# A quantised projection and a LoRA MLP on one core: gate/up and down as two-by-two block multiplications with seven block products

## The reference, cut to what matters

```python
# x: 8 x 256 x 1024, that is 2048 tokens of 1024; all float32
w_eff = quantise(weight + delta, codebook) * scale + delta      # 1024 x 1024, delta = lora_B @ lora_A / 2
x = x + x @ w_eff.T
gate = x @ W_gate.T + 0.5 * (x @ A_gate[idx].T) @ B_gate[idx].T  # W_gate, W_up: 2752 x 1024, rank 16
up   = x @ W_up.T   + 0.5 * (x @ A_up[idx].T)   @ B_up[idx].T    # idx: one adapter for each batch of 256 tokens
act  = silu(gate) * up
x = x + act @ W_down.T + 0.5 * (act @ A_down[idx].T) @ B_down[idx].T   # W_down: 1024 x 2752
```

## Time and profile before

| | |
|---|---|
| median of 3 runs | 1862.82 us (1861.52 to 1865.01) |
| span of the profiled execution | 1864.1 us; no other time is recorded for it |
| PE busy | 1810.1 us, 97% of the span |
| DVE busy | 746.1 us, 40% |
| ACT busy | 419.4 us, 22% |
| POOL busy | 72.6 us, 4% |
| DMA moved | 154.93 MB |

### The profile page before, as it was taken

How to read it: one execution, slowest core, us unless ns; L and a number is a source line. 1 busy time by engine, 2 the same in 40 slices (tenths; PEclk the granted TensorE clock), 3 DMA queues, 4 the chain that set the end, 5 groups by cost and what they waited for, 6 DMA issues and landing times. The chain is left out here.

```text
span 1864.1 us, 23210 instructions
## 1 busy us (share of the span) xinstructions
PE 1810.1 (97%) x8129; PEld 1466.2 (79%) x8129; DVE 746.1 (40%) x1261; ACT 419.4 (22%) x891; POOL 72.6 (4%) x76
## 2 busy tenths in 40 slices
PE   6799999999999999999999999999989999999998
PEld 5578877888888888888888888888776787778776
DVE  6989848533333333333333333332463111211221
ACT  5422243222222222122222222221232111111110
POOL 4820000000000000000000000000000000000000
PEclk9999999999999999999999999999999999999999
DMA  6584465111111111111111111110365243323431
GB/s 201 141 183 128 125 214 164 50 50 46 47 49 49 49 49 47 44 45 49 49 49 44 49 49 49 50 47 23 98 172 165 52 115 93 98 60 87 107 85 50
DMA packets 222225, 154.93 MB, mean 83 GB/s; under 512 B 92064, under 2 KB 193440, under 8 KB 222048
## 3 DMA queue, kind: packets, MB, share of 16 engines
q1 hardware_dynamic: 207680, 125.95, 25.3%
q10 hardware_dynamic: 12416, 22.55, 3.3%
q0 software_dynamic: 2080, 5.80, 1.6%
HBM read 102.34 MB, written 57.70 MB: 86 GB/s over the span
## 5 line engine op out<-in xcount | busy, mean ns | idle before, releaser
L1253 DVE TENSOR_TENSOR av<-bankU,sg 128x512 f32<-128x512 f32 x84 | 58.1, 691 | 561.8 <-PE bankU L1363 561.8
L1351 PE MATMUL bankG<-xh,wh 128*128 128x512 f32 x704 | 278.8, 396 | 1.6 <-PEq L290 1.6
L1688 PE MATMUL bankS<-dn_h,ah 128*128 128x512 f32 x704 | 279.7, 397 | 0.5 <-DVE ah L1635 0.5
L1688 PE MATMUL bankS<-dn_l,ah 128*128 128x512 f32 (+1 forms) x704 | 278.5, 396 | 0.0
L1351 PE MATMUL bankG<-xh,wl 128*128 128x512 f32 x704 | 275.5, 391 | 0.0
L1351 PE MATMUL bankG<-xl,wh 128*128 128x512 f32 x704 | 275.1, 391 | 0.0
L1688 PE MATMUL bankS<-dn_h,al 128*128 128x512 f32 x672 | 262.9, 391 | 0.0
L1351 PE MATMUL bankU<-xl,wh 128*128 128x512 f32 x672 | 262.2, 390 | 0.0
L1351 PE MATMUL bankU<-xh,wl 128*128 128x512 f32 x672 | 262.0, 390 | 0.0
L1351 PE MATMUL bankU<-xh,wh 128*128 128x512 f32 x672 | 262.0, 390 | 0.0
L1635 DVE TENSOR_TENSOR al<-a_raw,ah 128x256 fp32r<-128x256 f32 x168 | 71.0, 423 | 306.2 <-ACT ah L1572 306.1
(11 more groups left out here) (158 smaller groups left out, 1942.4 us busy)
## 6 DMA issues: line engine op xcount, KB each, us to landing
act_d<-av ACTq DMA_DIRECT2D x84, 256.0 KB, 2.4
a_raw<-act_d SPq DMA_DIRECT2D x168, 128.0 KB, 2.5
wn<-in_L_cond_W_gate_dram SPq DMA_DIRECT2D x84, 128.0 KB, 2.9
wn<-in_L_cond_W_up_dram SPq DMA_DIRECT2D x84, 128.0 KB, 2.8
wn<-in_L_cond_W_down_dram SPq DMA_DIRECT2D x42, 256.0 KB, 3.3
xnat<-in_x_dram SPq DMA_DIRECT2D x8, 1024.0 KB, 5.1
x1T_d<-x1t_st SPq DMA_DIRECT2D x32, 256.0 KB, 2.5
x_d<-x1n_st SPq DMA_DIRECT2D x32, 256.0 KB, 2.8
```

What stands on the lines that cost most here:

```text
L1253: dv.tensor_tensor(av[0:rows, :], up, sg[0:rows, :], ALU.mult).then_inc(s_av, 1)
L1351: te.matmul(bank[:, :], a[:, q, g, k, :], b[:, c, k, :], start=(k == 0 and n == 0), stop=False)
L1688: last = te.matmul(bank[par][NH * t + h][:, :], a[0:r, slot, tok], w[0:r, k, cols], start=(k == 0 and m == 0), stop=False)
```

## The change

Gate, up and down are each computed as a two-by-two block product with seven block products in place of eight. For gate and up the blocks are halves of the 2752 weight rows (1376 each: 11 tiles, the last of 96 rows), halves of the 1024 inputs, and two chunks of 512 tokens out of four. For down they are halves of the 2752 inputs, of the 1024 outputs and of the tokens. The block sums are made in float32 ahead of the split into high and low:

- Sums of x1's blocks (XS_d): on VectorE at the end of stage 1 for the first token half (`pair_sums`), on GpSimd in stage 2 for the second (`xt_sums`).
- Sums of weight blocks: four on GpSimd for every pass of seven products (`w_s12`, `w_s3`, `w_s4`).
- Sums of the act blocks (`act_sum`, four for two passes) and of W_down's blocks (`dn_sums`, four for each of 11 tiles) on GpSimd too. Act blocks and sums go to LT_d (seven operands), W_down's to RT_d.

A pass `mm` is one weight (gate for m = 0, up for m = 1) by one of 11 tiles by one half of the tokens: 44 passes, a pair is `it` (22). In a pass the position `p` counts the products; product p is 12 matmuls into its own bank, and four of the seven also get an adapter matmul. VectorE adds the banks up in SBUF (`ev`, L1405 to L1421), which it did not do before: silu and the product of gate and up then read SBUF. The split weights go through a ring of five (`rh`, `rl`); the weight transposes go to SBUF (`wt`). W_down is transposed by VectorE in stage 2 (`dn_tr`, L1389), so stage 3 has no transposes on TensorE. x1 is no longer transposed back in stage 1: VectorE transposes it from XR_d in stage 3 (`residual`, L1757). Stage 2 now loads its x1 operands from HBM, seven of 1 MB for each token half, which `x_hi` and `x_lo` split; in the first pass of each half TensorE also computes the adapters' inputs (`T`, 16 and 24 matmuls) and VectorE `make_ts`. The act buffer and W_down are read back in stage 3, in 14 runs of 11 steps; each run is a product for one half of the tokens, 12 matmuls a step, and `evict` adds its four banks into one to four blocks of the result, which is in SBUF throughout. The loops of stages 1 to 3 are now written out.

```diff
-                        for tt in range(TT):
-                            last = te.transpose(bankM[:, tt * P:(tt + 1) * P], x1t_st[:, c % 2, tt * P:(tt + 1) * P], ident[:, :])
-                        last.then_inc(s_trM, 1)
...
-                        for k in range(KD):
-                            if k % TT == 0 and c == 0 and not (isinstance(j, int) and j == 0):
-                                pe.wait_ge(s_lo, use(j, 2 * g + k // TT) + 1)
-                            for n, (a, b) in enumerate(((wh, xh), (wh, xl), (wl, xh))):
-                                te.matmul(bank[:, :], a[:, q, g, k, :], b[:, c, k, :], start=(k == 0 and n == 0), stop=False)
...
-                            for m in range(TT):
-                                last = te.transpose(bank[1][wbank(k, h)][0:r, m * P:(m + 1) * P], dn_n[:, h, m, 0:r], ident[:, :])
-                            last.then_inc(s_dntr, 1)
...
-                                    for m, (a, w, r) in enumerate(pairs):
-                                        last = te.matmul(bank[par][NH * t + h][:, :], a[0:r, slot, tok], w[0:r, k, cols],
-                                                         start=(k == 0 and m == 0), stop=False)
-                            last.then_inc(s_used, 1)
...
+            OUT = (bank1[:, :], bankA[:, 1, :], bankA[:, 0, :], bank7[:, :], bank5[:, :], bankC[:, 1, :], bankC[:, 0, :])
...
+                    def w_s12(mm):
+                        rows = rows_of(mm // 2 % NJ)
+                        gp.wait_ge(s_tr, 4 * mm + 3)
+                        wait(gp, s_lo, 7 * (mm - 1) + 5)
+                        tt(wsrc(S1, rows), wsrc(L21, rows), wsrc(L22, rows), ALU.add).then_inc(s_sum, 1)
+                        gp.wait_ge(s_sum, 4 * mm + 1)
+                        tt(wsrc(S2, rows), wsrc(S1, rows), wsrc(L11, rows), ALU.subtract).then_inc(s_sum, 1)
...
+                        gp.wait_ge(s_sum, 4 * mm + 2)
+                        tt(wsrc(L12, rows), wsrc(L12, rows), wsrc(S2, rows), ALU.subtract).then_inc(s_sum, 1)
...
+                            ins = tt(s1a[r, :], a12, a22, ALU.add)
...
+                            ins = tt(s2a[r, :], s1a[r, :], a11, ALU.subtract)
...
+                            tt(b11, b12, b11, ALU.subtract).then_inc(s_ds, 1)
...
+                    def hi(v):
+                        mm, p, it, m = split(v)
+                        rows = rows_of(it % NJ)
+                        s, n = ((s_tr, 1), (s_sum, 2), (s_tr, 4), (s_sum, 3), (s_sum, 1), (s_tr, 3), (s_sum, 4))[p]
+                        act.wait_ge(s, 4 * mm + n)
+                        wait(act, s_pd, v - RING + 1)
+                        nc.scalar.copy(rh[:, v % RING, 0:KH * rows], wsrc(RSRC[p], rows)).then_inc(s_hi, 1)
...
+                        dv.transpose(wsrc(n, rows), src).then_inc(s_tr, 1)
+                    def lo(v):
+                        mm, p, it, m = split(v)
+                        rows = rows_of(it % NJ)
+                        dve.wait_ge(s_hi, v + 1)
+                        dv.tensor_tensor(rl[:, v % RING, 0:KH * rows], wsrc(RSRC[p], rows),
+                                         rh[:, v % RING, 0:KH * rows].bitcast(f32), ALU.subtract).then_inc(s_lo, 1)
...
+                        dv.transpose(dt_[r, b, :], src.rearrange("p a r -> p (a r)")).then_inc(s_dtr, 1)
...
+                                dv.tensor_tensor(e[:, 0:2, :], bankA[r, :, :], tm[r, None, :].to_broadcast([r.stop, 2, CH]),
+                                                 ALU.add).then_inc(s_ev, 1)
...
+                                dv.tensor_tensor(e[:, 2, :], bank7[r, :], e[:, 1, :], ALU.add).then_inc(s_ev, 1)
...
+                                dv.tensor_tensor(e[:, 1:4:2, :], bank5[r, None, :].to_broadcast([r.stop, 2, CH]), e[:, 1:3, :],
+                                                 ALU.add).then_inc(s_ev, 1)
...
+                                dv.tensor_tensor(e[:, 1:3, :], bankC[r, :, :], e[:, 1:3, :], ALU.add).then_inc(s_ev, 1)
...
+                    def product(u, ks, first, signal):
+                        mm, p, it, m = split(u)
+                        rows = rows_of(it % NJ)
+                        last = None
+                        for k in ks:
+                            cols = slice(k * rows, (k + 1) * rows)
+                            for n, (a, b) in enumerate(((rh, xh), (rh, xl), (rl, xh))):
+                                last = te.matmul(OUT[p][0:rows, :], a[:, u % RING, cols], b[:, OPND[p], k, :],
+                                                 start=first and k == ks[0] and n == 0,
+                                                 stop=k == KH - 1 and n == 2 and p in (0, 1, 3))
...
+            PORD = (M7, M5, M6, M1, M2, M4, M3)
+            C11, C12, C21, C22 = range(4)
+            TARGETS = {M7: (C21, C22), M5: (C12, C22), M6: (C12, C21, C22), M1: (C22, C11, C12, C21),
+                       M2: (C11,), M4: (C21,), M3: (C12,)}
...
+            RES_RUN = (8, 8, 4, 4, 4, 4)
...
+                    for k in range(NJ):
+                        load_r(0, k)
+                        if k < NL:
+                            load_l(k)
+                        if k == NL:
+                            sp.dma_start(td[:, :, :].bitcast(f32), TD_d.rearrange("c p n -> p c n")).then_inc(s_td, 16)
+                            for n in range(4):
+                                sp.dma_start(bd[n * CR:(n + 1) * CR, :, :].bitcast(f32),
+                                             BdT_d[n // 2].rearrange("(c r) d -> r c d", r=CR)).then_inc(s_bd, 16)
...
+                    def load_res(n):
+                        q, h, t = RES[n]
+                        wait(act, s_res, n - 1)
+                        for g in range(NI):
+                            for e in range(2):
+                                i = 2 * (q % 2) + e
+                                act.dma_start(xs[g * Q:(g + 1) * Q, n % 2, e * KD:(e + 1) * KD, :],
+                                              XR_d[2 * h + q // 2, :, i * Q:(i + 1) * Q, t * P + g * Q:t * P + (g + 1) * Q]
+                                              .rearrange("o c r -> c o r")).then_inc(s_xs[n % 2], 16)
...
+                    nres = 0
+                    for k in range(NJ):
+                        r_hi(0, k)
+                        if k < NL - 1:
+                            l_hi(k)
+                    act.wait_ge(s_bd, 64)
+                    nc.scalar.activation(bdn[:, :, :], bd[:, :, CH:D].rearrange("p (h t) n -> p h t n", t=2)[:, :, 1, :].bitcast(f32),
+                                         ACT.Copy, scale=-1.0).then_inc(s_bdn, 1)
...
+                        dv.transpose(c_tile(q, h, t), xs[:, n % 2, :, :].rearrange("p b r -> p (b r)")).then_inc(s_res, 1)
...
+                        for q in TARGETS[PORD[r // 2]]:
+                            c = c_tile(q, r % 2, t)
+                            ins = dv.tensor_tensor(c, bank[r % 2][t][:, :], c, ALU.add)
+                        ins.then_inc(s_ev, 1)
...
+                    pe.wait_ge(s_td, 16)
+                    pe.wait_ge(s_bdn, 1)
+                    for n in range(NJ * NRUN):
...
+                            for i, (a, b) in enumerate(((lh, rh), (lh, rl), (ll, rh))):
+                                last = te.matmul(out_, a[0:rows, n % NL, tok], b[0:rows, k, :],
+                                                 start=(k == 0 and i == 0), stop=(k == NJ - 1 and i == 2 and not adds))
...
```

More of the change, by code:

```diff
@@ L398, in _ @@
                     tile(0)
-                    with sp.Fori(0, 2) as i:
+                    for i in range(2):
                         tile(2 * i + 1)
@@ L693, in _ @@
                     adapters(0)
-                    with dve.Fori(0, 2) as i:
+                    for i in range(2):
                         for q in (0, 1):
@@ new lines, in lora @@
+                    def lora(u):
+                        mm, p, it, m = split(u)
+                        h, rows = it // NJ, rows_of(it % NJ)
+                        half, t = {2: (0, 0), 4: (1, 1), 5: (1, 0), 6: (0, 1)}[p]
+                        pe.wait_ge(s_ts, 2 * h + t + 1)
+                        pe.wait_ge(s_bs[m], 128 * (it + 1))
+                        te.matmul(OUT[p][0:rows, :], bs[:, m, t, half * P:half * P + rows], ts[:, t, m, :],
+                                  start=False, stop=True).then_inc(s_pd, 1)
@@ new lines, in _ @@
+                    for n in range(NJ * NRUN):
+                        r, k = n // NJ, n % NJ
+                        if n + NL < NJ * NRUN:
+                            load_l(n + NL)
+                        if r % 2 == 1 and r // 2 + 1 < NRUN // 2:
+                            load_r(r // 2 + 1, k)
+                        if r - 1 in FINAL and k in (2, 4, 6, 8):
+                            store(r - 1, k // 2 - 1)
+                    for t in range(TT):
+                        store(NRUN - 1, t)
@@ new lines, in _ @@
+                    for k in range(NJ):
+                        r_lo(0, k)
```

(16 more changed lines are left out.)

1609 lines of the change are left out of this document (835 added, 774 removed).

## The result

The changed kernel takes 1968.34 us (median of 4 runs, 1964.68 to 1970.33) against 1863.36 (4 runs, 1861.52 to 1865.01): ratio 1.056, 95% interval 1.054 to 1.058. It is 5.6% slower; 1748 was forecast, so the forecast is 220 us off and on the wrong side. The profiled execution took 1963.1 us.

What follows compares the result with a forecast made beforehand. It took the time as a count of TensorE instructions: 256 + 49 + 2 + 928 + 20 + 12 = 1267 us to stage 2's end, + 41 + 3 + 424 + 8 + 5 = 1748, 6.2% faster; range 1700 to 1832.

Steps and rivals of the forecast that it cites:

- TensorE's count: Matmuls at 0.2247 us each: 4128 in stage 2 (928 us) and 1888 in stage 3 (424 us).
- Loss 49: Seam into stage 2: 78 us to the end of pass 0, its matmuls worth 29; bounds 25 and 65.
- Store and barrier 5: Seam into stage 2: storing x1's last block and the barrier behind it take 5 us.
- 20 us lost: Between the token halves: operand work and masking of adapter sums fall on two passes; bounds 5 and 35.
- I charge 12 us over the whole stage: Stage 2: 12 us for pairs in which VectorE's and GpSimd's bursts don't fit together.
- 8 us of ring: Stage 2: five weight slots let VectorE be late by three products, 8 us.
- 41 us: Seam into stage 3: additions, `td`, store, barrier and the wait for `bdn`, where there were 3.7; bounds 30 and 55.
- the neighbour: GpSimd beside VectorE in stage 2: each GpSimd instruction costs VectorE 0.55 us; bank readers would go free.
- B: Rival, stage 2: VectorE partly the bound, 3 to 5 us more for 15 pairs, 1800 to 1830; chance 0.22.
- D: Rival, stage 2: each GpSimd instruction delays VectorE 1.08 us, bank readers and transposes too; 171 us, 1907 in all; chance 0.08.
- That seven products don't show: Rival: matmuls stand further apart as 12 in place of 24 go to a bank between waits; no difference, 0.01.
- The signs I had named: Stage 2: right, 440 or more matmuls in 100 us; wrong, under 420 with TensorE waiting for L1307, or slowed bank readers.

Runs made afterwards that it cites:

- kernel 1: The changed kernel with each down-adapter step `td` one product later on TensorE: 1858.69 us, ratio to before 0.997.
- Kernel 4: The changed kernel with x operands and the second load of A issued earlier on SyncE at the start of stage 2: 1952.41 us.
- Kernel 11: kernel 5 plus Kernel 4's order, the down stage's adapter operands loaded in the eighth step, the residual's loads issued by GpSimd: 1797.33 us, ratio to before 0.966.
- kernel 2: The changed kernel with GpSimd's block sums in stage 2 narrowed to 8 columns after the first passes, result incomplete: 1905.39 us.
- kernel 6: kernel 1 with GpSimd's block sums of stage 2 narrowed to 8 columns after the first passes, result incomplete: 1819.82 us.
- kernel 13: The changed kernel with five more matmuls ahead of each `td` outside the first and the middle pass: 1963.51 us.
- kernel 5: kernel 1 with all work on W_down (loads, transposes, sums, stores) four products later: 1816.03 us, ratio to before 0.976.

## Why the prediction was wrong

The forecast missed the profiled 1963.1 us by 215. Where they are, step by step, with a matmul at 0.2247 us:

- **TensorE's count** (4128, or 928 us, for stage 2 and 1888, or 424 us, for stage 3) was right, and so was its price: 442 start in 100 us in kernel 1.
- **Stage 1** ended its matmuls at 260.4, forecast 256: 4 us.
- **"Loss 49"** for the seam into stage 2 (51 with the clock): 79, so 28 us. Two terms were too small. "Store and barrier 5": from the last matmul of stage 1 (260.4) to the first load of stage 2 (280.54) 20 us pass, in which SyncE still loads and stores for the sums of x1's blocks. No run here touched it. And SyncE's order: I had the queue as a list of issues in time and not as instructions that wait. `store_bs` waits for `bh` and `bl`, the weight load of pass 2 for a transpose, and x and A stand behind them. Kernel 4 shows 16 us of it.
- **"20 us lost"** between the token halves: 100 us with 265 matmuls lose 40, so 20 us. 18.9 of the 40 are again `td`'s waits for `al`, up to 6.3 us long. Kernel 11 still loses 38 there, mostly in waits for `ts`, A and `al`, and no run was aimed at it: its cause stays open.
- **"I charge 12 us over the whole stage" is the step that failed.** Steady stage 2, from 400 to 860 and from 960 to 1478, has 978 us for 3610 matmuls worth 811: 167 us lost, 155 above the charge. The charge compared each engine's load in a pair with 41.3 us (and its own upper ends, 42 and 43 us, are above that). The loads fit, and VectorE stayed at 68%. But `td` is an instruction in TensorE's order with a chain of six steps on VectorE and ScalarE behind the product ahead of it, and one product, 2.8 us, to cover it; the prediction put this wait at nothing. "8 us of ring" is true of the weights and of no use here: the ring lies ahead of a product, `td` behind one. Of the 167, 105 are the waits for `al` in these two stretches. The rest is an estimate: the granted clock of 0.97 and 0.95 is worth about 0.03 x 460 + 0.05 x 518 = 40, and 58 stops that each end the overlap of two matmuls (one lasts 0.39 us, they start 0.225 apart) and begin with a slow one (0.47) about 0.25 each, 15. That makes 160 of 167.
- **"41 us"** for the seam into stage 3 was forecast from the last product on, with 6 us for its additions, splits and `td`. So the wait for `bdn` (41.5, from the last `td`) is not what to hold against it: from the last product (its last matmul starts at 1475.3) to stage 3's first matmul (1525.75) it is some 49 us, within the bounds. The rest of stage 3 took 437 us for 440. From 1478 on the two together are 4 us over.

With 2 us lost between 380 and 400 these make 213 of the 215. Kernel 1 shows the mechanism: one line of order, no work less, 110 us. Kernels 2 and 6 show what the neighbour adds (63 and 39 us), and kernel 13 what slow matmuls behind the stops add (some 29) to waits that the order makes. With `td` one product later and W_down's work moved, steady stage 2 loses 19 us in kernel 11 (400 to 760 and 860 to 1310, 810 us for 3519 matmuls): the charge of 12 was nearly right for a kernel in which this chain is covered.

The rivals: none had this place. *B* named waits in order on ScalarE and SyncE that make VectorE late, 3 to 5 us for 15 pairs; measured are about 8 per pair, on all pairs, and it is TensorE's own order. *D*, slower, had the sign, and its 171 us for stage 2 lie next to the 167 measured, but that is luck: it fell by its own test, as bank readers and transposes are not slowed. The neighbour was priced too high: `rl` has a mean of 0.838, forecast 0.9 to 1.1, and kernel 2, which narrows some 300 sums, takes only 73 us off VectorE's busy time (1274.8 to 1202.2), 0.24 per sum and not 0.55. By the rule of the Trainium skill, page "SBUF — State Buffer", section "SBUF: two separate sides", a bank reader goes free beside GpSimd; the trace agrees, L1421 takes 1.225 us with the sums in full and 1.225 in kernel 2. "That seven products don't show", by a longer distance of matmuls, is refuted by kernel 1. The signs I had named were read rightly in one respect: fewer than 420 in 100 us was to mean wrong, but with TensorE waiting for L1307; that wait is 2.3 us in sum.

On *GpSimd for elementwise sums*: in the changed kernel they cost 63 us (kernel 2), against kernel 1 39 us (kernel 6), and with W_down's work moved 17.7 us of waits are left with every sum in place (kernel 5, 436 in 100 us). The Trainium skill, page "GPSIMD Engine Reference", section "Engine selection", advises against such sums on GpSimd, as about twice slower; the trace agrees on the price, 1.3 us each and more beside VectorE (means of 1.29 to 1.75 by line) against VectorE's 0.69. In this kernel it cost time where a chain without slack ran beside them.

So the change itself had the sign that was forecast for it, once the order was right: with `td` one product later, W_down four later, x ahead and the down stage's start reordered it is 3.4% faster than before. What separates kernel 11 (1795.5 profiled) from 1748 is 3 us in stage 1, 16 at the seam into stage 2 (67 lost from 260 to 380 us, forecast 51), 18 between the token halves, 7 in steady stage 2 and 2 from the last product on.

## What to carry to other kernels

Comparing each engine's load with the period says only that a steady state is possible. For every instruction that an in-order engine carries between its main work, write down when its last input is ready, step by step along the engines' own orders, and when the engine reaches it; here one product of cover left 131.6 us of waits, two left 50.4, most of it where a burst and a busy neighbour met, and moving W_down's work left 17.7. And read a DMA queue as a program with waits in it: what is issued behind a waiting store starts when the store does.

## What the runs showed of the hardware

- Stops of TensorE of 1 to 2.2 us left the granted clock at 1.00 in one stretch (400:500). Elsewhere one of 2.01 us (646.64) was followed by some 3 us of matmuls 0.43 us apart, and kernel 2 has 0.97 in its own 400:500 with stops of 2.01 us at most. One of 3.06 us was followed by 5.7 us at 0.50. In kernel 13, filling and shortening the stops gave back some 29 us beyond their length.
- GpSimd's addition of 128x512 float32 takes 1.30 us alone and up to 1.73 in the rows shown beside VectorE, and VectorE's of two SBUF inputs 0.69 alone and up to 1.78 beside it: both pay, and two such steps in a row took 1.56 and 1.76 us, 1.9 more than alone. Transposes (0.707 with full and with narrowed sums) and bank readers (1.225 with both) on VectorE don't pay.
- Pieces of 128 bytes fill the DMA engines (share 0.98) at 215 GB/s together with large loads; with seven eighths of them gone the share is 0.84 at 200 GB/s, and TensorE's 50 matmuls in 20 us are 70.
